# A three-layer graph network kernel: sorted edges and gathered sums replaced by unsorted edge tiles and accumulating DMAs into DRAM

## What is computed

```python
def _sage_conv(x, src, dst, Wp, bp, Wl, bl, Wr):
    h = jax.nn.relu(x @ Wp.T + bp)
    agg = jax.ops.segment_sum(h[src], dst, num_segments=N)
    cnt = jax.ops.segment_sum(jnp.ones((src.shape[0],), x.dtype), dst, num_segments=N)
    agg = agg / jnp.maximum(cnt, 1.0)[:, None]
    return agg @ Wl.T + bl + x @ Wr.T

h = jnp.maximum(_layernorm(x, axis=-1), 0.0)
...
x = _sage_conv(x, src, dst, Wp0, bp0, Wl0, bl0, Wr0)
x = _relu_ln(x, g0, be0)
x = _sage_conv(x, src, dst, Wp1, bp1, Wl1, bl1, Wr1)
x = _relu_ln(x, g1, be1)
x = _sage_conv(x, src, dst, Wp2, bp2, Wl2, bl2, Wr2)
```

## Time and profile before

| | us |
|---|---|
| median of 3 runs | 1790.1 |
| lowest, highest | 1789.18, 1793.37 |
| profiled execution, span from first to last instruction | 1787.6 |
| PE busy | 1702.4 (95%) |
| DVE busy | 1330.3 (74%) |
| ACT busy | 706.4 (40%) |
| POOL busy | 488.4 (27%) |

### The profile page before, as it was taken

The page is one execution under the profiler, slowest core; times in us unless marked ns, Lnnn a source line. Parts: engine busy times, 40 slices in busy tenths (PEclk is TensorE's granted clock), DMA queues, the critical chain, the costliest instruction groups (busy, mean ns, idle before and its releaser), DMA issues.

```text
span 1787.6 us, 32256 instructions
## 1 busy us (share of the span) xinstructions
PE 1702.4 (95%) x8594; PEld 1384.0 (77%) x8594; DVE 1330.3 (74%) x3334; ACT 706.4 (40%) x1470; POOL 488.4 (27%) x768
## 2 busy tenths in 40 slices
PE   5779999997999998999999899998999999999999
PEld 3568888875777776888887788886888888788887
DVE  7968888867999985767675888885766776566665
ACT  3344444436888883222222444442322222111111
POOL 5421111103333332111101333333111110344443
PEclk9889999998999999999999999999999999999999
DMA  3022222116777762422212777775222221799997
GB/s 131 24 71 77 77 70 76 65 60 203 236 238 232 235 206 83 159 76 76 76 62 85 259 243 245 242 245 175 71 77 76 76 76 48 266 333 323 328 323 260
DMA packets 131639, 280.99 MB, mean 157 GB/s; under 512 B 17559, under 2 KB 17559, under 8 KB 131594
## 3 DMA queue, kind: packets, MB, share of 16 engines
q1 hardware_dynamic: 103034, 186.84, 30.1%
q0 software_dynamic: 28560, 93.61, 17.7%
HBM read 187.02 MB, written 93.36 MB: 157 GB/s over the span
## 4 chain that ended last, share of the span: by engine, by line
PE 83%; DVE 6%; DMA 5%; issue 3%; ACT 2%; SPq 1%; DVEq 0%; POOL 0%; ACTq 0%; POOLq 0%
PE bank L616 23%; PE bank L618 22%; PE bank L617 22%; PE bank L788 5%; PE bank L741 3%; PE bank L758 3%; DMA x_tile<-x 3%; PE bank L756 3%; DMA x_tile<-node_x 1%; DVE y L1285 1%; DVE ln_stats L1112 1%; DVE in_stats L1112 1%; ACT y L944 1%; ACT y L937 0%; DMA gathered<-node_x,gather_idx 0%
## 5 line engine op out<-in xcount | busy, mean ns | idle before, releaser
L616 PE MATMUL bank<-w_high_r,xt_low 128*128 128x512 f32 x948 | 395.8, 418 | 6.3 <-DVE xt_low L1134 3.9
L618 PE MATMUL bank<-w_high_r,xt_high 128*128 128x512 f32 x948 | 375.2, 396 | 0.0
L617 PE MATMUL bank<-w_low_r,xt_high 128*128 128x512 f32 x948 | 375.2, 396 | 0.0
L924 ACT ACTIVATE xt_high<-bank 128x512 fp32r<-128x512 f32 x237 | 141.4, 597 | 359.6 <-PE bank L788 347.0
L602 POOL DMA_INDIRECT edge_row<-edge_table,owner_idx x237 | 230.5, 973 | 95.2 <-POOL owner_idx L582 49.3
L582 POOL COPY owner_idx<-owner 128x1 int32 (+1 forms) x237 | 72.7, 307 | 520.8 <-DVE y L1289 210.8
L618 PEld LDWEIGHTS bank<-w_high_r,xt_high 128*128 128x128 f32 x948 | 179.1, 189 | 42.8
L892 ACT ACTIVATE agg_high<-agg 128x512 fp32r<-128x512 f32 x120 | 75.9, 632 | 342.8 <-DVE agg L1187 337.6
L616 PEld LDWEIGHTS bank<-w_high_r,xt_low 128*128 128x128 f32 x948 | 179.9, 190 | 39.9 <-issue 7.4
L1289 DVE TENSOR_TENSOR y<-bank,edge_row 128x512 f32<-128x512 f32 x158 | 109.2, 691 | 131.1 <-PE bank L618 102.4
L617 PEld LDWEIGHTS bank<-w_low_r,xt_high 128*128 128x128 f32 x948 | 180.3, 190 | 32.8
(11 more groups left out here) (167 smaller groups left out, 3090.6 us busy)
## 6 DMA issues: line engine op xcount, KB each, us to landing
node_x<-y SPq DMA_DIRECT2D x158, 256.0 KB, 3.3
x_tile<-node_x SPq DMA_DIRECT2D x158, 256.0 KB, 4.9
edge_table<-edge_out SPq DMA_DIRECT2D x120, 256.0 KB, 2.0
x_tile<-x SPq DMA_DIRECT2D x78, 256.0 KB, 3.4
residual<-x SPq DMA_DIRECT2D x78, 256.0 KB, 5.1
out<-y SPq DMA_DIRECT2D x78, 256.0 KB, 5.6
edge_row<-edge_table,owner_idx POOLq DMA_INDIRECT x237, 4.2
stage_p<-Wp_t SPq DMA_DIRECT2D x3, 1024.0 KB, 5.7
```

The costliest lines, as they stand in the source:

```text
L616: nc.tensor.matmul(psum, a_low[:, k, :], w_high[m][:, k, :], start=(k == 0), stop=False)
L617: nc.tensor.matmul(psum, a_high[:, k, :], w_low[m][:, k, :], start=False, stop=False)
L618: last = nc.tensor.matmul(psum, a_high[:, k, :], w_high[m][:, k, :], start=False, stop=(k == K - 1))
L924: nc.scalar.activation(xt_high[:, slot].rearrange("p k m -> p (k m)"), bank[slot][:], turned_act).then_inc(n_xt_high, 1)
```

## The change

The program is written anew and fully unrolled.

- **No sort.** The host lays src and dst out in 40 tiles of 125 edges, in the given order. POOL makes one-hot tiles, PE counts edges per node during the first node phase (`count`), POOL fetches each edge's count by indirect DMA, and DVE takes the reciprocal (`share`). DVE's `rank` finds, inside a tile, the edges that aren't the first with their dst; `places` sends those rows to 128 spare rows behind the table.
- **Node phase first.** For each tile: load, ReLU (ACT, from layer 1 on), layer norm (DVE and ACT), store of the normed rows `xn` in `node_x`, transposes, product with Wr, plus bias, store as z in `node_z` (in the last layer plus residual, into `out`).
- **Edge phase after it.** POOL gathers rows of `node_x`. For four tiles together (a group, 500 edges) PE computes h with blocks of Wp stationary and the features streaming, 500 columns at a time, so h comes out transposed. Then for each tile it multiplies by Wl (12 matmuls) and sums equal dst by 2 matmuls of 512 columns. ACT scales by the share, and POOL adds the 128 rows to `node_z` (or `out`) with an accumulating indirect DMA. Each such DMA waits until the one before has landed (`e_added`).
- **Between layers.** SP waits for the last accumulating DMA before it loads the first node tile of the next layer. Biases of the folded layer norm come from `shift_p` and `shift_z`.

The functions of the node and edge steps, the order of the steps on each engine, and POOL's DMAs:

```diff
+AHEAD_RELU = 7
+AHEAD_STATS = 6
+AHEAD_MEAN = 5
+AHEAD_XN = 4
+AHEAD_TURN = 2
...
+            def gather(l, t):
+                slot = t % IN_RING
+                if t >= IN_RING:
+                    pool.wait_ge(e_turned, l * EDGE_TILES + t - IN_RING + 1)
+                G.indirect_dma_start(
+                    out=rows_in[:, slot, :], out_offset=None, in_=node_x,
+                    in_offset=bass.IndirectOffsetOnAxis(ap=src_i[:, t:t + 1], axis=0)
+                ).then_inc(e_gathered[slot], DMA)
...
+                pool.wait_ge(e_out, e + 1)
+
+                if e:
+                    pool.wait_ge(e_added, DMA * e)
+                G.indirect_dma_start(
+                    out=node_z if l + 1 < LAYERS else out,
+                    out_offset=bass.IndirectOffsetOnAxis(ap=into_i[:, t:t + 1], axis=0),
+                    in_=rows_out[:, slot, :], in_offset=None, compute_op=ALU.add
+                ).then_inc(e_added, DMA)
...
+            def project(l, g, m):
+                h = l * EDGE_TILES + g * GROUP + m
+                if m == 0:
+                    pe.wait_ge(e_xt_low, l * EDGE_TILES + (g + 1) * GROUP)
...
+                for s in range(EDGE_TILES):
+                    g, i = s // GROUP, s % GROUP
+                    if g + 1 < GROUPS:
+                        project(l, g + 1, i)
+                    edge_product(l, s)
+                    if s >= 1:
+                        edge_sum(l, s - 1)
+                    if s + 2 * GROUP < EDGE_TILES:
+                        edge_turn(l, s + 2 * GROUP)
+                edge_sum(l, EDGE_TILES - 1)
...
+                for i in NODE_STEPS:
+                    if is_node(i + AHEAD_TURN):
+                        node_xt_high(l, i + AHEAD_TURN)
+                    if l and is_node(i + AHEAD_RELU):
+                        node_relu(l, i + AHEAD_RELU)
+                    if is_node(i + AHEAD_MEAN):
+                        node_std(l, i + AHEAD_MEAN)
+                    if is_node(i + AHEAD_XN):
+                        node_norm(l, i + AHEAD_XN)
...
+                for s in range(EDGE_TILES):
+                    g, i = s // GROUP, s % GROUP
+                    if g + 1 < GROUPS:
+                        h_high_of(l, g + 1, i)
+                    p_high_of(l, s)
+                    if s >= 1:
+                        edge_out(l, s - 1)
+                    if s + 2 * GROUP < EDGE_TILES:
+                        edge_xt_high(l, s + 2 * GROUP)
...
+                for i in NODE_STEPS:
+                    if is_node(i + AHEAD_TURN):
+                        node_xt_low(l, i + AHEAD_TURN)
+                    if is_node(i - 1):
+                        node_out(l, i - 1)
+                    if is_node(i + AHEAD_STATS):
+                        node_stats(l, i + AHEAD_STATS)
+                    if is_node(i + AHEAD_MEAN):
+                        node_mean(l, i + AHEAD_MEAN)
+                    if is_node(i + AHEAD_XN):
+                        node_rstd(l, i + AHEAD_XN)
+                        node_off(l, i + AHEAD_XN)
```

More of the change, by code:

```diff
@@ L37, with sage_kernel @@
 LAYERS = 3
-CONSTS = 12
 DMA = 16
[L40 to L80, removed]
+CONSTS = 6
+IN_RING = 8
+XN_RING = 4
+XT_RING = 3
+OUT_RING = 4
+RES_RING = 4
+ROW_RING = 4
+HOT_RING = 4
+GROUP = 4
+AHEAD_RELU = 7
[3 more added lines that the diff above has]
+AHEAD_TURN = 2
+STEP_SPLIT_P = 4
+STEP_SHIFT_P = 10
+STEP_LOAD_L = 14
+STEP_SPLIT_L = 30
+STEP_SHIFT_COLS = 8
+STEP_SPLIT_R = 12
+STEP_COUNTED = 44
+STEP_SHARE = 70
+def sage_kernel(nc, x_in, src_cols, dst_cols, dst_rows, weights, out):
     N, D = x_in.shape
-    E = src_in.shape[0]
+    EDGE_TILES, EDGE_ROWS = dst_rows.shape
     K = D // P
@@ L246, in sage_kernel @@
+        h_high = sb("h_high", [P, 2, K, GROUP_ROWS], F32R)
+        h_low = sb("h_low", [P, 2, K, GROUP_ROWS], F32R)
+        p_high = sb("p_high", [P, 2, D], F32R)
+        p_low = sb("p_low", [P, 2, D], F32R)
+        stats = sb("stats", [P, IN_RING, 6], F32)
+        mean = sb("mean", [P, IN_RING, 2], F32)
+        std = sb("std", [P, IN_RING], F32)
+        rstd = sb("rstd", [P, IN_RING], F32)
+        off = sb("off", [P, IN_RING], F32)
         consts = sem("consts")
-        memset_done = sem("memset_done")
@@ L364, in all_edge_rows_stored, with turns, uses @@
-        def all_edge_rows_stored(eng, l):
-            for s in range(EDGE_RING):
-                eng.wait_ge(e_stored[s], DMA * (l + 1) * (-(-(EDGE_TILES - s) // EDGE_RING)))
-        def all_nodes_stored(eng, l):
-            for s in range(NODE_RING):
-                eng.wait_ge(n_stored[s], DMA * (l + 1) * (-(-(NODE_TILES - s) // NODE_RING)))
+        e_added = sem("e_added")
+        def turns(t, ring):
+            return t // ring + 1
+        def uses(count, ring, slot):
+            return -(-(count - slot) // ring)
@@ L502, in _ @@
+            G.memset(ones[:], 1.0).then_inc(ones_done, 1)
+            pool.wait_ge(ones_done, 1)
             triangle(ident, ALU.is_equal)
             triangle(below, ALU.is_gt, -1)
[L504 to L509 removed]
@@ L699, in _ @@
-            sweep(pe, EDGE_TILES, STEP, 0, 1, rank_step)
-            def sort_chunk(j, c, first, last):
-                pe.wait_ge(placed_done, j * CHUNKS + (c + 1))
-                for i in range(CHUNK):
-                    slot = c * CHUNK + i
-                    done = nc.tensor.matmul(bank[4][:, 0:3 * EDGE_TILES], place[:, slot, :], placed[:, slot, :],
-                                            start=first and i == 0, stop=last and i == CHUNK - 1,
-                                            skip_group_check=True)
-                done.then_inc(sorted_chunk, 1)
@@ new lines, in node_rstd, with node_off @@
+            def node_rstd(l, t):
+                slot = t % IN_RING
+                dve.wait_ge(n_std, l * NODE_TILES + t + 1)
+                V.reciprocal(rstd[:, slot:slot + 1], std[:, slot:slot + 1]).then_inc(n_rstd, 1)
+            def node_off(l, t):
+                slot = t % IN_RING
+                dve.wait_ge(n_rstd, l * NODE_TILES + t + 1)
+                V.scalar_tensor_tensor(out=off[:, slot:slot + 1], in0=mean[:, slot, 0:1], scalar=-1.0,
+                                       in1=rstd[:, slot:slot + 1], op0=ALU.mult, op1=ALU.mult).then_inc(n_off, 1)
```

1578 lines of the change are left out of this document (626 added, 952 removed).

## The result

The changed kernel takes 1883.8 us (median of 4 runs, 1878.7 to 1885.2) against 1789.6 in the same session: ratio 1.051, 95% interval 1.049 to 1.054. The forecast was 1807. So the sign was right, and 77 us of loss were missing from the sum. The time lies outside the forecast's own range of 1775 to 1835. It lies inside 1715 to 1890, but that range was made wide for rivals A and B, and neither came true, so this is luck. The profiled execution has a span of 1883.5 us.

The account below looks back on a forecast made before the run. PE phases behind a setup bound the old kernel. Start 17, node phases 867, edge phases 846, gaps 57 and end 17 gave a span of 1804, so 1807 us against 1790; own range 1775 to 1835, with rivals 1715 to 1890.

Parts of the forecast that it names:

- A: Node step: PE sets it, not waits between ACT and DVE; 222 turns give back 0.40 us each, 1718 us; chance 0.15.
- B: Edge phase: the accumulating DMA is dear, 7.5 us each, every phase grows by 33 us, 1905 us; chance 0.15.
- Part 1: Start: 91 us of setup give way to 17 us of pipeline filling; counting, ranks and one-hots cost nothing while engines have room.
- Part 2: Node step: ACT and DVE wait for each other in a ring of 3.62 us, above PE's 3.22; 867 us for three layers.
- Part 3: Edge step: 6.49 us instead of 6.91, but a 1.9 us stall at each group's border; 282 us a phase, 846 for three.
- Part 4: Accumulating DMAs: 5.4 us each, between 3.4 and 7.5, hidden under PE's edge steps except at the end, 15.6 us.
- Part 5: Between layers: PE idles 28.6 us, 15.6 for the last DMAs plus 13 for load and pipeline, twice, 57 us.
- C: Group borders in edge phases: idle time halves PE's clock, 27 borders cost some 1.5 us each, 40 us, 1847; chance 0.10.
- D: Small terms add up in favour: node step 3.5, DMA 3.6 to 4.5, stalls 1.4 us; 1747 us; chance 0.15 with mixtures.

Follow-up runs that it names:

- Pairs: Changed kernel with POOL's 40 small gathers of edge_count issued two per node step instead of in one unbroken row: 1845.7 us against 1884.
- my first edit: Changed kernel with ACT's norm of a node tile one step later, SP's store and reload moving with it: 2045.3 us, 161 us slower.
- bursts of ten: Changed kernel with the 40 small gathers of edge_count in four bursts, five node steps apart: 1855.2 us against 1884.

## Why the prediction was right and wrong

**Part 1, the step that failed.** The filling of the pipeline was sized well (19.3 for 17). What failed is the sentence that counting, ranks and one-hots "cost nothing while that holds", namely while their engines have room: POOL had room (27% busy in both kernels), and its row of 40 gathers cost 40 us. POOL's busy share was the wrong thing to ask. I had costed the 40 gathers as work on POOL and didn't ask what a long row of issues does to others, and no row of before shows such a row. Pairs and the kernel without gathers both give the 40 us back. This is half of the miss. None of the signs that I had named for being wrong appeared (steps near 3.2, DMAs over 7, edge phases more than 10 us from 282), so the list had no place for it. The ranks did cost next to nothing: the steps beside them (31.8 to 175.5 us) are 3.57 to 3.58 except where pieces of weights are split.

**Part 2** was right in mechanism and size: 3.57 for 3.62 us, confirmed by its removal (3.23). One link was named wrongly. ACT's idle time stands before std, ended by the moments, and not before the norm, ended by `off`; both end within 0.3 us of each other on DVE, so the size didn't suffer, but my first edit did. Two terms were missing from the sum: POOL's addition in the last layer (16 us, shown by leaving it out) and the bias matmuls (some 4 us in each of two layers). The middle layer's phase came out 4 us below my 289 in spite of its bias matmuls, because a turn took 3.57 for 3.62 and 13 of the first 20 steps ran at PE's pace (3.23 to 3.26).

**Part 3** was right: 6.43 for 6.49, and a stall of 1.7 to 1.8 for 1.9, shown by moving the tiles ahead. Mis-sized was the time until four tiles are split at the phase's start: 4.75 forecast, 9 to 10.4 measured. In the changed kernel and its twelve variants, the 8 starts whose row of gathers is broken after eight take 4.7 to 5.2 us, and the other 31, with ten to twelve in a row, 6.3 to 10.7. In the third layers a part of that is waiting for the gathers themselves (7.1 us in three waits in the changed kernel). So that the row is the cause fits all starts, but it was argued and not tried by itself.

**Part 4** was right: 5.45 for 5.4 us. Without accumulation 3.47, the lower bound of 3.4. **Part 5**: 31.9 and 31.0 for 28.6; the last of the DMAs was issued at 650.47, 14.2 us after the last sum, and landed some 5 us later, where I had 15.6 for both. The rest, 12.7, is the 13 of the forecast. The half clock is there (0.61 in the gap).

**The rivals.** A (PE sets the step): no, but it became true with the short instructions first. B (dear DMA): no. C (borders halve the clock): no, the clock in edge phases is 0.98, and a matmul behind the stall shows 0.50 once and then the usual 0.39. D: no.

So of the 77 us missing, 40 are the row of small gathers, 16 the addition on POOL, 14 the starts of the edge phases, and the rest small terms with both signs.

## What to carry to other kernels

When work moves to an engine with room, ask how its instructions stand in a row and whose operands they touch, not only how busy it is: in this kernel a row of ten or more indirect DMA issues on POOL without a pause belonged into pairs between other work. When two in-order engines wait for each other in each step, draw the whole cycle with every instruction between the two waits, and put the short ones whose operands are a step old at the front. An edit that moves one end of a ring must be drawn again as a ring, since the next engine may close a longer one.

## What wasn't expected of the hardware

- A row of indirect DMAs on POOL, one every 1.15 to 1.25 us, holds PE up after about ten of them, whether each moves 16 or 128 elements. First ACT learns late of PE's finished transposes (its xt_high comes 5.5 us behind them instead of 3.43 in bursts of ten, 19 and 43 us in the row of 40). In the long row PE's matmuls slow down too, to one every 1.4 to 2.8 us instead of 0.23, and the granted clock falls to 0.50 with it. By what path POOL does this is open. The trace gives no sign that PE waits for its code: the instruction packets of queue 8, which by their rhythm are PE's, come 28 us apart before (177.3, 205.1), and the next at 273.4 is late by just the 40 us that PE lost. No run here tells whether plain DMAs issued by POOL do the same.
- A POOL addition of 128 x 512 stretched a 128 x 1 DVE instruction from 0.16 to as much as 1.18 us.
- A block of 16 one-column matmuls, with PE busy throughout, was followed by a granted clock of 0.66 over 5 us in one layer and not in another of the same kernel.
